# First attention: probabilities scaled by the inverse sums on GpSimd before they are transposed

## What is computed

```
xn, latn = layernorm(ctx), layernorm(layernorm(x))      # 256 rows each
q = latn @ Wq                                           # 16 heads of 64
k, v = split(concat([xn, latn]) @ Wkv)                  # 512 keys
weight = softmax((q * s) @ (k * s).T)                   # 256 x 512 for each head
out = (weight @ v) @ Wo
```

## Time and profile before

| what | value |
|---|---|
| median of 3 runs | 1862.97 us (1862.88 to 1864.71) |
| span of the profiled execution | 1861.9 us |
| first attention | to about 731 us of the span |
| TensorE busy, whole span | 1577.6 us, 85% |
| VectorE busy | 1130.7 us, 61% |
| ScalarE busy | 938.2 us, 50% |
| GpSimd busy | 508.7 us, 27% |
| busy in 300 to 385 us (the attention): TensorE, VectorE, ScalarE, GpSimd | 79.76, 63.62, 60.33, 8.42 of 85 us |
| granted TensorE clock in 300 to 385 us | 1.00 |

### The profile page before, as it was taken

How to read it: one execution, slowest core, us unless ns; L and a number is a source line. 1 busy time by engine, 2 the same in 40 slices (tenths; PEclk the granted TensorE clock), 3 DMA queues, 4 the chain that set the end, 5 groups by cost and what they waited for, 6 DMA issues and landing times. The chain is left out here.

```text
span 1861.9 us, 30273 instructions
## 1 busy us (share of the span) xinstructions
PE 1577.6 (85%) x9776; PEld 1250.2 (67%) x9776; DVE 1130.7 (61%) x2274; ACT 938.2 (50%) x2305; POOL 508.7 (27%) x385
## 2 busy tenths in 40 slices
PE   4999999999999996369995935999996569999967
PEld 3778777777777785336664824767664448888856
DVE  6887777777778765413332365776776644444447
ACT  2776766767676774311112214666564144444432
POOL 6111010101010100410004035565561034444424
PEclk9999999999999998579997967999999589999989
DMA  4200000000000000089982010000000023333313
GB/s 125 88 1 13 1 12 2 13 2 13 1 13 1 1 1 1 34 298 312 320 293 91 1 29 17 7 13 6 6 1 1 1 61 106 108 103 120 104 54 114
DMA packets 66508, 115.78 MB, mean 62 GB/s; under 512 B 6256, under 2 KB 46192, under 8 KB 66384
## 3 DMA queue, kind: packets, MB, share of 16 engines
q1 hardware_dynamic: 61440, 99.66, 16.5%
q0 software_dynamic: 4944, 14.55, 2.2%
HBM read 97.68 MB, written 16.52 MB: 61 GB/s over the span
## 5 line engine op out<-in xcount | busy, mean ns | idle before, releaser
L435 ACT ACTIVATE a_p<-a_s,a_negmax 128x512 f32<-128x512 f32 x256 | 176.0, 688 | 157.5 <-DVE a_negmax L603 115.9
L603 DVE TENSOR_REDUCE a_negmax<-a_s 128x1 f32<-128x512 f32 x256 | 176.0, 688 | 47.0 <-PE a_s L298 36.9
L207 POOL TENSOR_TENSOR a_o_l<-a_o,a_o_h 128x256 fp32r<-128x256 f32 x64 | 47.0, 735 | 559.6 <-ACT a_o_h L460 559.6
L1545 ACT ACTIVATE h_probs<-h_scores,h_negmax 128x256 f32<-128x256 f32 x256 | 119.1, 473 | 91.9 <-DVE h_negmax L1738 91.3
L2160 POOL TENSOR_TENSOR n_w_l<-n_raw,n_w_h 128x768 fp32r<-128x768 f32 x64 | 118.3, 1849 | 148.7 <-ACT n_w_h L2130 148.7
L307 PE MATMUL a_t<-ident,a_p 128*128 128x128 f32 x1024 | 156.9, 276 | 0.7 <-DVE a_pT L618 0.7
L307 PEld LDWEIGHTS a_t<-ident,a_p 128*128 128x128 f32 x1024 | 120.7, 140 | 52.9 <-issue 17.9
L597 DVE TENSOR_TENSOR a_k_hl<-a_k_p,a_k_hl 64x512 fp32r<-64x512 f32 x128 | 88.2, 689 | 71.6 <-ACT a_k_hl L418 70.6
L325 PE MATMUL a_out_p<-a_pT,a_v 128*64 128x256 f32 x1024 | 124.6, 385 | 0.0
L1738 DVE TENSOR_REDUCE h_negmax<-h_scores 128x2 f32<-128x512 f32 x128 | 86.5, 685 | 60.9 <-PE h_scores L1605 59.5
L297 PE MATMUL a_s<-a_k_hl,a_q_hh 128*128 128x512 f32 x256 | 108.2, 423 | 9.3 <-ACT a_p L435 7.6
(11 more groups left out here) (357 smaller groups left out, 4761.9 us busy)
## 6 DMA issues: line engine op xcount, KB each, us to landing
e_w_in<-in_L_ffn_gate_up_proj SPq DMA_DIRECT2D x31, 1024.0 KB, 6.2
n_raw<-in_L_ffn_w SPq DMA_DIRECT2D x64, 384.0 KB, 3.0
e_w_out<-in_L_ffn_down_proj SPq DMA_DIRECT2D x31, 512.0 KB, 4.2
chosen_out<-n_result POOLq DMA_DIRECT2D x16, 256.0 KB, 4.5
u_y<-chosen_out SPq DMA_DIRECT2D x8, 512.0 KB, 4.0
rows_in<-a_zeros SPq DMA_DIRECT2D x1, 3968.0 KB, 15.7
...
```

The costliest lines, as they stand in the source:

```text
L435: act.activation(probs[j][:, :], scores[j % 2][:, :], ACT.Exp, bias=negmax[:, j:j + 1], accum_out=total[:, r % 2, j % 2, j // 2:j // 2 + 1 ...
L603: dve.tensor_reduce(negmax[:, j:j + 1], scores[j % 2][:, :], AX.X, ALU.max, negate=True).then_inc(max_set, 1)
L1545: ins = act.activation(probs[u % 4][:, h, :], scores[u % 2][:, h, :], ACT.Exp, bias=negmax[:, u % 4, h:h + 1], accum_out=total[:, (u // 4) ...
```

## The change

The sums are now inverted tile by tile: `invert(b, r, j)` on VectorE (128 x 1) stands behind the next maximum. GpSimd multiplies `probs[j]` in place by the inverse, repeated along 512 columns (`normalise`), and sets `shares_set`; `turn` waits for that in place of the exponential. With the result scaled already, `spread`, the two transposes of the inverses, the copy and the multiplication of `set_out` go; `high_o` reads the product in PSUM, right at the end of the step in which it is made, and `low_o` moves to VectorE as a subtraction from PSUM. `out_p` has one half. `project_out` and `add` move from r = 2 to r = 1, and `project_out` stands ahead of `attend`. In the diff, declarations of semaphores, the calls of `spread` and the work behind the last batch are left out.

```diff
@@ -114,14 +114,12 @@
-        negmax, total, inverse = sb("a_negmax", [P, 4]), sb("a_total", [P, 2, 2, 2]), sb("a_inverse", [P, 2, 2, 2])
-        inverses = [sb(f"a_inverses{i}", [P, 2, 2, DH]) for i in range(2)]
-        inverse_T, o_full = sb("a_inverse_T", [P, S]), [sb(f"a_o{i}", [P, S]) for i in range(4)]
+        negmax, total, inverse = sb("a_negmax", [P, 4]), sb("a_total", [P, 4]), sb("a_inverse", [P, 4])
         o_h, o_l = sb("a_o_h", [P, PAIRS, S], F32R), sb("a_o_l", [P, PAIRS, S], F32R)
...
         turned_p = [psum(f"a_t{i}", [P, NC, P]) for i in range(2)]
-        out_p, k_p, v_p = psum("a_out_p", [P, 2, S]), psum("a_k_p", [P, N]), psum("a_v_p", [P, 2, 2 * P])
+        out_p, k_p, v_p = psum("a_out_p", [P, S]), psum("a_k_p", [P, N]), psum("a_v_p", [P, 2, 2 * P])
@@ -202,9 +200,11 @@
-                def low_o(b, r):
-                    pool.wait_ge(oh_set, PAIRS * b + r + 1)
-                    pool.tensor_tensor(o_l[:, r, :], o_full[r % 4][:, :], o_h[:, r, :], ALU.subtract).then_inc(ol_set, 1)
+                def normalise(b, r, j):
+                    pool.wait_ge(inv_set, 4 * (PAIRS * b + r) + j + 1)
+                    pool.tensor_tensor(probs[j][:, :], probs[j][:, :], inverse[:, j:j + 1].to_broadcast([P, N]),
+                                       ALU.mult).then_inc(shares_set, 1)
@@ -223,12 +223,12 @@
                     for r in range(PAIRS):
+                        normalise(b, r, 0)
+                        normalise(b, r, 1)
                         if r in (5, 6) and last < 2:
                             low_kv(b + 1, 1 - bp, r - 5)
-                        if r >= 2:
-                            low_o(b, r - 2)
-                        elif not first:
-                            low_o(b - 1, PAIRS + r - 2)
+                        normalise(b, r, 2)
+                        normalise(b, r, 3)
@@ -300,7 +298,7 @@
                     s = PAIRS * b + r
-                    pe.wait_ge(exp_set, 4 * s + j + 1)
+                    pe.wait_ge(shares_set, 4 * s + j + 1)
@@ -313,16 +311,12 @@
                     pe.wait_ge(v_set, s + 2 - r % 2)
-                    pe.wait_ge(spread_set, s + 1)
-                    wait(pe, o_set, s)
-                    for half in range(2):
-                        pe.transpose(out_p[:, 1, half * P:(half + 1) * P], inverses[r % 2][:, half, :, :], g.ident[:, :])
+                    wait(pe, ol_set, s)
                     for c in range(NC):
...
                             at = r % 2 * P + h * DH
-                            ins = pe.matmul(out_p[h * DH:(h + 1) * DH, 0, :], v[r // 2 % 2][:, c, at:at + DH],
+                            ins = pe.matmul(out_p[h * DH:(h + 1) * DH, :], v[r // 2 % 2][:, c, at:at + DH],
                                             probsT[r % 2][h][:, c, :], start=(c == 0), stop=(c == NC - 1))
@@ -355,7 +349,7 @@
-                            if r == 3:
+                            if r == 2:
                                 wait(pe, added, b)
@@ -368,12 +362,12 @@
                         score(b, r, 3)
+                        if r == 1 and not first:
+                            pe.wait_ge(ql_set, PAIRS * b + r + 2)
+                            project_out(b - 1)
                         if prev:
...
                         turn(b, r, 1)
-                        if r == 2 and not first:
-                            pe.wait_ge(ql_set, PAIRS * b + r + 2)
-                            project_out(b - 1)
                         if r in (4, 5) and last < 2:
@@ -431,19 +425,9 @@
-                    wait(act, inv_set, PAIRS * b + r - 1)
+                    wait(act, inv_set, n - 3)
                     act.activation(probs[j][:, :], scores[j % 2][:, :], ACT.Exp, bias=negmax[:, j:j + 1],
-                                   accum_out=total[:, r % 2, j % 2, j // 2:j // 2 + 1]).then_inc(exp_set, 1)
-                def spread(b, r):
-                    s = PAIRS * b + r
-                    act.wait_ge(inv_set, s + 1)
-                    wait(act, o_done, s - 1)
-                    act.activation(inverses[r % 2][:, :, :, :],
-                                   inverse[:, r % 2, :, :].unsqueeze(3).to_broadcast([P, 2, 2, DH]),
-                                   ACT.Copy).then_inc(spread_set, 1)
+                                   accum_out=total[:, j:j + 1]).then_inc(exp_set, 1)
@@ -453,11 +437,11 @@
                 def high_o(b, r):
-                    act.wait_ge(o_set, PAIRS * b + r + 1)
+                    act.wait_ge(o_done, PAIRS * b + r + 1)
                     if r == 0:
...
                         wait(act, y_done, b)
-                    act.activation(o_h[:, r, :], o_full[r % 4][:, :], ACT.Copy).then_inc(oh_set, 1)
+                    act.activation(o_h[:, r, :], out_p[:, :], ACT.Copy).then_inc(oh_set, 1)
@@ -484,10 +466,8 @@
                             set_v(b + 1, 0, r % 2)
-                        if r >= 2:
-                            high_o(b, r - 2)
-                        elif not first:
-                            high_o(b - 1, PAIRS + r - 2)
+                        if prev:
+                            high_o(*prev)
@@ -603,12 +581,12 @@
-                def invert(b, r):
-                    s = PAIRS * b + r
-                    dve.wait_ge(exp_set, 4 * s + 4)
-                    wait(dve, spread_set, s - 1)
-                    dve.reciprocal(inverse[:, r % 2, :, :], total[:, r % 2, :, :]).then_inc(inv_set, 1)
+                def invert(b, r, j):
+                    n = 4 * (PAIRS * b + r) + j
+                    dve.wait_ge(exp_set, n + 1)
+                    wait(dve, shares_set, n - 3)
+                    dve.reciprocal(inverse[:, j:j + 1], total[:, j:j + 1]).then_inc(inv_set, 1)
@@ -617,14 +595,9 @@
-                def set_out(b, r):
-                    s = PAIRS * b + r
-                    dve.wait_ge(o_done, s + 1)
-                    wait(dve, ol_set, s - 3)
-                    dve.tensor_copy(inverse_T[:, :], out_p[:, 1, :]).then_inc(invT_set, 1)
-                    dve.wait_ge(invT_set, s + 1)
-                    dve.tensor_tensor(o_full[r % 4][:, :], out_p[:, 0, :], inverse_T[:, :], ALU.mult).then_inc(o_set, 1)
+                def low_o(b, r):
+                    dve.wait_ge(oh_set, PAIRS * b + r + 1)
+                    dve.tensor_tensor(o_l[:, r, :], out_p[:, :], o_h[:, r, :], ALU.subtract).then_inc(ol_set, 1)
@@ -640,24 +613,27 @@
                         if prev:
-                            invert(*prev)
+                            invert(*prev, 3)
                         between(r, 0)
                         maximum(b, r, 1)
+                        invert(b, r, 0)
                         if nxt:
...
                         maximum(b, r, 2)
+                        invert(b, r, 1)
                         if nxt:
...
                         maximum(b, r, 3)
+                        invert(b, r, 2)
+                        set_odd(b, r, 1)
                         if prev:
-                            set_out(*prev)
-                        set_odd(b, r, 1)
+                            low_o(*prev)
                         between(r, 3)
-                        if r == 2 and not first:
+                        if r == 1 and not first:
                             add(b - 1)
```

16 lines of the change are left out of this document (5 added, 11 removed).

## The result

The changed kernel takes **1982.26 us** (median of 4 runs, 1978.46 to 1989.0) against 1863.84 for the kernel before, measured beside it (1862.88 to 1867.2). The ratio is 1.063, with a 95% interval of 1.061 to 1.066: slower by 118 us.

A forecast was written before the change was run, and what follows sets the result against it. First attention bound by TensorE in bare steps, by VectorE in steps with preparation; 6.5 + 5.6 + 34 + 29 + 1.3 + 9 + 12 = 97 us on 1861.9, plus 1, gives 1960 us, range 1900 to 1990.

The forecast's parts named there:

- Rival (c): Dearer: the multiplication takes 1.27 us, some 14 us more, and the clock falls twice as long: 1986; chance 0.12.
- start (r0 of batch 0): First transposes wait until about 50.5 us for GpSimd's weight splits and first normalisation: +9 us.
- step 6, seven batches, with the clock: In r = 6, V waits for the low half behind GpSimd's normalisations, +34 us; clock falls after long waits, +12.
- r1 and r2, batches 1 to 6: Output projection moves to r = 1, leaving VectorE's preparation in r = 2 uncovered: 29.9 us against 25.1, +29 in all.
- r1 and r2, batch 0 and last: The projection's move costs 1.3 us for batch 0, where r = 2 was bare before; nothing for the last.
- r3 and r4, batches 0 to 6: Transposes 2 and 3 wait behind delayed maxima, about 10.6 us a step in place of 10.31: +5.6 us.
- bare steps: Steps without preparation: transposes 0 wait 0.62 us, 0.31 is saved, 9.69 us in place of 9.38: +6.5 us.
- The multiplication: GpSimd's scaling of 512 columns takes 1.05 us, by the row of a mask multiplication; 0.9 to 1.27 as ends.
- Rival (b): Only what queue orders force: the projection's move is free and the clock holds, 55 us slower, 1918; chance 0.20.
- one subtraction of about 0.45 us: On VectorE it and three more reciprocals replace a copy and multiplication of 0.8 us; chain some 0.1 us shorter.
- GpSimd blocking VectorE: VectorE's SBUF-to-SBUF preparation stands still while GpSimd works: up to 0.5 us a step, included in the other figures.

The follow-up runs named there:

- experiment 1: Changed kernel with GpSimd's low half of the next batch's inputs behind the first normalisation in r = 5 and 6, not the second: 1940.44 us.
- experiment 10: Changed kernel with the splits of three weight pieces moved from ahead of the first multiplication into seven chunks over steps 0 to 6 of batch 0: 1975.62 us.
- Experiment 3: Changed kernel with GpSimd multiplying only columns 0 to 255 of each probability tile, half of the softmax's division left out: 1973.65 us.
- experiment 8: Changed kernel with experiments 1, 4 and 5 together, K ahead of transposes 2 and V ahead of transposes 0 on TensorE: 1866.61 us.
- Experiment 4: Changed kernel with VectorE's subtraction for the result's low half moved behind the next step's first maximum and reciprocal: 1945.78 us.
- Experiment 2: Changed kernel with the output projection back in r = 2, still ahead of the product, and an extra slot for pair 0's result: 1982.52 us.
- experiment 5: Changed kernel with the output projection in r = 2 and behind transposes 1, with the extra slot for pair 0's result: 1971.91 us.
- experiment 7: Kernel before the change with the output projection of r = 2 moved ahead of the product: 1903.98 us.
- experiment 12: Changed kernel with everything mended, weight splits in chunks over batch 0, and the places of K, V and chunks chosen by step: 1852.99 us.

## Why the prediction came out as it did

The forecast of 1960 us had the direction, the causes of the greater part and the size within 22 us. Rival (c) had 1986, nearer to the measured 1982, but not by its reasons: the multiplication took 1.04 us and not 1.27. (Its own sum, 1961 + 26, is also 1 off.) Its terms against the steps' lengths in the two traces:

| term | forecast, us | measured, us |
|---|---|---|
| start (r0 of batch 0) | 9 | 9.3 |
| step 6, seven batches, with the clock | 34 + 12 | 46.2 |
| r1 and r2, batches 1 to 6 | 29 | 34.8 |
| r1 and r2, batch 0 and last | 1.3 and 0 | 1.7 and 2.2 |
| r0, batches 1 to 6 | 0 | 4.9 |
| r3 and r4, batches 0 to 6 | 5.6 | 11.8 |
| bare steps | 6.5 | 7.4 |
| sum (of the unrounded) | 97 | 118.2 |

- **The multiplication: right.** 1.04 us, forecast 1.05 from the mask's row. By the Trainium skill, GPSIMD Engine Reference, section 3.1, the estimate was 1.3; the measurement decides for the row.
- **The start and step 6: right**, in mechanism (experiments 1 and 10) and size. V was forecast 9.07 us behind the first maximum and came at 9.11, 5.0 later than before; V and score 3 at the lower clock add 1.4 (2.73 and 0.66 us for 1.51 and 0.46), and some 0.2 come back behind them: 6.2 us more in batch 2. The forecast had 4.8 and 1.7. In batches 0 and 6 the clock lay low for twice as long, and step 6 lost 7.3 and 7.4 us. The clock fell at the start too, behind the wait of 11.52 us, where no term had it: the first transposes came at 50.09 (forecast 50.5), 12.1 us late, and cost 9.3. V's passes there lost 1.2 us by the clock alone, so the other work made up for 4 us or more, not for 3.5; that these two misses cancel is luck. Rival (b), by which the clock would hold and the projection's move be free, is refuted on both.
- **Bare steps: right in size, less so in place.** Forecast 9.69, measured 9.75. The wait isn't one of 0.62 us ahead of transposes 0 but is spread over several places (in the step from 800.22, 0.31 us ahead of transposes 3, 0.14 ahead of transposes 0 and 0.10 ahead of the product). Experiment 3 shows it to be the relay's, experiment 8 that order cures it.
- **r3 and r4: the step that failed** is the removed-and-added one, "one subtraction of about 0.45 us". Its duration was right (0.42), its wait was costed at nothing: moved from GpSimd to VectorE, it stands in a list where maxima are behind it, and waits up to 0.95 us for ScalarE, whose own list holds it behind an exponential and a copy. That is also the term missing for r = 0. Experiment 4 has it, at 36 us in all, more than the terms of r0, r3 and r4 together: r = 2 is in it too, and r = 0 of batch 2 fell to 11.15, below the 11.35 of the kernel before.
- **The projection's move: right size by a wrong reason.** 34.8 for 29. The forecast blamed the step: preparation in r = 2 without cover. Experiment 2 refutes this, since moving back gave nothing. What held is the forecast's own length of the two steps, 17.4 and 12.5, measured 17.9 and 13.0; what it missed is that the same cover is lost in r = 2, as soon as VectorE stands in a wait behind the projection (experiments 5 and 7, 5.26 and 8.29 us). Only with the subtraction out of the way and the projection behind transposes 1 are r = 1 and 2 together 25.2 us again, the 25.1 of the kernel before.
- **GpSimd blocking VectorE** was charged with up to 0.5 us in r = 2. VectorE's small operations of the preparation take 0.9 to 1.0 us more in each of r = 1 to 4 of a middle batch (63.4 us in place of 38.0 over the attention). But the steps did not pay for it: in experiment 3 the excess is 0.4 us a step, and they are shorter by 0.05 at most; in experiment 12 it is 0.7 to 1.3, and r = 1, 3 and 4 of a middle batch are shorter than in the kernel before.
